# Normalisations laid between the low parts of q and k, row maxima ten steps ahead instead of eight, ten of sixteen moves on GpSimd, and block 6 transposed by VectorE

## The reference

```python
xn = _layernorm(x)
q, k, v = split(xn @ w_qkv);  q, k = spectral_filter(q, mask), spectral_filter(k, mask)
attn = softmax(q @ k.T / 4)                       # 2 batches x 16 heads, 2048 x 2048 each
a = (attn @ v) @ w_out + b_out
y = square(relu(xn @ W_fc.T)) @ W_proj.T          # then 5 steps: mem = 0.9*mem + y - reset
return x + a + mean_of_spikes(y)
```

## Time and profile before

| | |
|---|---|
| median of 3 runs | 1691.74 us (1691.41 to 1691.75) |
| the profiled execution | 1691.07 us, its span 1689.3 us |
| busy in the span | PE 1681.4, PEld 1145.9, DVE 1494.2, ACT 1330.1, POOL 719.7 us |
| granted TensorE clock | 1.00 of full speed |
| first pass, TensorE | 12.09 to 111.37 us |
| score loop | 112.80 to 1658.6 us |
| output projection | 1658.6 us to the end |

### The profile page before, as it was taken

One profiled execution on the slowest core, in us unless ns is written; L12 is line 12 of the kernel. 1 busy time (PEld: TensorE's weight loads), 2 busy tenths in 40 slices (PEclk: granted clock), 3 DMA queues, 4 the chain that ended last, 5 costly groups with the idle time before them and its releaser, 6 DMA issues.

```text
span 1689.3 us, 44435 instructions
## 1 busy us (share of the span) xinstructions
PE 1681.4 (100%) x17842; PEld 1145.9 (68%) x17842; DVE 1494.2 (88%) x2375; ACT 1330.1 (79%) x1718; POOL 719.7 (43%) x979
## 2 busy tenths in 40 slices
PE   9999999999999999999999999999999999999999
PEld 6566666666666666666666666666666666666667
DVE  6889999998999999989998999999989998999884
ACT  5548888888888888888888888888888888888872
POOL 3103334555433345554333455543335554333455
PEclk9999999999999999999999999999999999999999
DMA  6851122112211221122112211221122112211133
GB/s 216 294 161 47 33 54 55 51 33 55 55 50 34 55 55 43 41 55 55 43 41 55 56 37 47 55 55 36 48 55 56 31 53 55 55 30 54 43 105 103
DMA packets 95406, 108.02 MB, mean 64 GB/s; under 512 B 56032, under 2 KB 70240, under 8 KB 95200
## 3 DMA queue, kind: packets, MB, share of 16 engines
q1 hardware_dynamic: 91744, 101.97, 21.2%
q10 hardware_dynamic: 3456, 3.21, 0.6%
HBM read 78.91 MB, written 20.97 MB: 59 GB/s over the span
## 4 chain that ended last, share of the span: by engine, by line
PE 98%; DVE 1%; ACT 0%; issue 0%; ACTq 0%; POOL 0%; POOLq 0%
PE banks L735 31%; PE ring L711 22%; PE ring L718 14%; PE ring L724 14%; PE banks L841 7%; PE banks L846 3%; PE banks L659 2%; PE ring L928 2%; PE ring L672 1%; PE ring L645 1%; PE ring L659 1%; PE ring L686 0%; DVE stats L947 0%; DVE attnT L979 0%; ACT xnT L513 0%
## 5 line engine op out<-in xcount | busy, mean ns | idle before, releaser
L562 ACT ACTIVATE probs<-ring 128x1024 f32<-128x1024 f32 x1024 | 1002.1, 1026 | 6.5 <-PE ring L724 6.2
L711 PE MATMUL ring<-kst,qst 64*128 64x512 f32 x2000 | 674.7, 417 | 0.3 <-ACT probs L562 0.3
L735 PE MATMUL banks<-probs,vst 128*32 128x256 f32 x8192 | 548.2, 385 | 0.1
L1036 DVE TENSOR_REDUCE pmax<-ring 128x2 f32<-128x1024 f32 x407 | 497.7, 1223 | 12.7 <-PE ring L711 0.5
L568 ACT ACTIVATE half_sb<-ring 128x512 f32<-128x512 f32 x500 | 299.2, 598 | 261.4 <-PE ring L711 254.1
L718 PE MATMUL ring<-qst,kst 64*128 64x512 f32 x2048 | 493.0, 425 | 0.1
L711 PEld LDWEIGHTS ring<-kst,qst 64*128 64x128 f32 x2000 | 328.3, 184 | 208.3 <-issue 204.6
L1017 DVE TENSOR_REDUCE pmax<-ring 128x1 f32<-128x512 f32 x500 | 345.4, 691 | 88.7 <-PE ring L711 85.1
L724 PE MATMUL ring<-shift_rows,ones 64*128 64x512 f32 x2048 | 422.9, 390 | 0.0
L1023 DVE TENSOR_REDUCE pmax<-half_sb 128x1 f32<-128x512 f32 x500 | 335.5, 671 | 37.0 <-ACT half_sb L568 33.1
L735 PEld LDWEIGHTS banks<-probs,vst 128*32 128x32 f32 x8192 | 213.7, 109 | 209.7 <-issue 91.0
(11 more groups left out here) (96 smaller groups left out, 1050.9 us busy)
## 6 DMA issues: line engine op xcount, KB each, us to landing
kst<-qk_scratch SPq DMA_DIRECT2D x256, 128.0 KB, 3.0
qst<-qk_scratch SPq DMA_DIRECT2D x256, 128.0 KB, 2.9
qk_scratch<-attnT SPq DMA_DIRECT2D x32, 256.0 KB, 3.0
shift_rows<-shiftT SPq DMA_DIRECT2D x512, 2.0 KB
qk_scratch<-probs SPq DMA_DIRECT2D x16, 256.0 KB, 3.0
attnT<-o_turned SPq DMA_DIRECT2D x256, 16.0 KB, 1.9
xnT<-x SPq DMA_DIRECT2D x8, 512.0 KB, 5.6
out<-xnT SPq DMA_DIRECT2D x7, 512.0 KB, 2.9
```

The source lines that it names most:

```text
L562: act.activation(probs[:, s % PS, :], score_slot(g), ACT.Exp, scale=SCALE).then_inc(exp_done, 1)
L711: return pe.matmul(unit_slot(g)[:, c * BLK:(c + 1) * BLK], qst[b][rows, tile * P:(tile + 1) * P], kst[b][rows, key:key + BLK], start=True, ...
L735: mm = pe.matmul(po[32 * j:32 * (j + 1), half * D:(half + 1) * D], vst[b][:, kt, :], quarters[:, j], start=(kt == 0), stop=(kt == TB - 1))
L1036: dve.tensor_reduce(pmax[:, tile, 2 * part:2 * part + 2], unit_slot(g).rearrange("p (c e) -> p c e", c=2), AX, ALU.max).then_inc(mx_taken, 1)
```

## The change

Five edits in one.

- `LEAD` becomes 10. The first pass takes 44 maxima instead of 48 (`first_max` does nothing from 44 on), and in the last head one more pair, `s` = 8, has maxima. `split_shift` stays at `s` = 10 and 26; `turn_output` goes from 12 and 28 to 14 and 30.
- `TURNED` takes in block 6: VectorE transposes it, and TensorE does so only for blocks 0 and 7.
- `MOVES` becomes (0, 2, 2, 2): ScalarE moves 6 pieces of each such block, GpSimd 10.
- In blocks 1 to 4 the normalisation of block `t + 2` is laid behind the four low parts, the transposition behind the last. Block 0 still normalises block 2 at its end, and block 4 still block 7.
- ScalarE takes the root for block `t + 2` behind high copy 1 in blocks 1 to 4.

```diff
-LEAD = 8
+LEAD = 10
...
-TURNED = range(1, 6)
-MOVES = (0, 2, 3, 3)
+TURNED = range(1, 7)
+MOVES = (0, 2, 2, 2)
...
-                    if t == 4 and w == 1:
-                        deviation(6)
+                    if 1 <= t <= 4 and w == 1:
+                        deviation(t + 2)
                     if t + 1 in TURNED and MOVES[w]:
                         move_turned(t + 1, w)
                 if t < NB - 1 and t + 1 not in TURNED:
                     take_transposed(t + 1)
-                if t < 4:
-                    deviation(t + 2)
+                if t == 0:
+                    deviation(2)
...
             def first_max(n):
+                if n >= FIRST_MAX:
+                    return
...
                     low_part(t, w)
-                    if t == 4 and w < 3:
-                        (block_stats, block_rstd, block_scale)[w](6)
-                if t < 4:
-                    normalise(t + 2)
+                    if 1 <= t <= 4 and (w < 3 or t + 2 in TURNED):
+                        (block_stats, block_rstd, block_scale, turn_block)[w](t + 2)
+                if t == 0:
+                    normalise(2)
...
-            halve(1, pmax[:, TB // 2:TB, 0:2], FIRST_MAX)
+            halve(1, pmax[:, TB // 2:FIRST_MAX // 2 - TB // 2, 0:2], FIRST_MAX)
...
-                if s == LEAD + 2:
+                if s == LEAD:
                     for link in range(4):
-                        split_shift(link, 2 * i + 1, 1, FIRST_MAX + g - 2)
+                        split_shift(link, 2 * i + 1, 1, FIRST_MAX + g)
                 if s == LEAD + 4 and i:
                     turn_output(2 * i - 1)
...
-                if s == LEAD + TB + 2 and not last:
+                if s == LEAD + TB and not last:
                     for link in range(4):
-                        split_shift(link, 2 * i + 2, 0, FIRST_MAX + g - 2)
+                        split_shift(link, 2 * i + 2, 0, FIRST_MAX + g)
                 if s == LEAD + TB + 4:
                     turn_output(2 * i)
```

More of the change, by code:

```diff
@@ L1186, in head @@
                             end_bias_of(t)
-                    if last and s == LEAD + TB:
+                    if last and s == TB + 8:
                         for t in END_LATE:
                             end_bias_of(t)
-                    if last and LEAD + TB < s <= LEAD + TB + 12:
-                        end_base_of((s - LEAD - TB) // 2 - 1)
+                    if last and TB + 8 < s <= TB + 20:
+                        end_base_of((s - TB - 8) // 2 - 1)
             for h in range(H - 1):
```

## The result

The changed kernel takes 1694.45 us in the median of 22 runs (1691.79 to 1695.59), the kernel before 1691.41 in 22 runs on the same chip (1690.69 to 1692.11). The ratio is 1.0016 with a 95% interval of 1.0010 to 1.0022: slower by about 2.7 us, 3.0 by the medians, where I had forecast no change and a range that ended at 1693.6. The profiled execution took 1693.99, its span is 1692.2 against 1689.3.

The account below looks back on a forecast made before the run. TensorE bounds the kernel, 98% of its chain, so only its work and waits count. Reduction +0.92, transposes -0.38, maxima -0.92, last head +0.23 and shift +0.1 sum to -0.05: 1691.7 us, range 1689.7 to 1693.6.

Parts of the forecast that it names:

- Block 2 gets its wait: First pass: block 2 waits for a chain of VectorE and ScalarE work and starts at 34.5 against 33.38, +1.1.
- Eight transposes of block 6: First pass, v of block 5: TensorE drops 0.87 of transposes but 0.49 of cover goes too, -0.38.
- the four maxima: First pass: four maxima less, 0.23 each, -0.92.
- that term: Last head: the shift's transfers land at 1638.5, pair 16 asks at 1638.46, a tie costed at +0.1 (0 to 0.5).
- VectorE reaches the first maxima later: First pass: the first reduction starts at 70.15, `first_max(2)` moves by +0.92, and TensorE's wait grows from 1.44 to about 2.1.
- the third rival: First pass: GpSimd's moves slow down beside VectorE, block 2 starts 2.7 later, reduction +2.6, 1694.3; chance 0.07.
- ends in that wait: First pass: all of the interleaving's gain is lost in TensorE's wait at `first_max(2)`, as block 7's normalisation stays undivided.
- The last head: Last head: pair 8 gets maxima, pairs 8 and 10 take 5.60 instead of 5.37, +0.23 (0 to 0.48).
- The sum: Whole kernel: 0.92 - 0.38 - 0.92 + 0.23 + 0.1 = -0.05, giving 1691.7.
- the forecast's own range: Whole kernel: 1690.1 to 1693.4 for the main forecast, which had chance 0.72.
- The base of the forecast: Whole kernel: the profiled execution's 1691.07, with the median of the runs 0.67 above it.

Follow-up runs that it names:

- the version without them: The changed kernel with block 6 transposed by TensorE again, so no moves lie beside block 7's normalisation: 1691.06 us, ratio 1.0002 to the kernel before.
- the moves held back: The changed kernel with GpSimd's ten moves of block 6 held until block 7 is normalised: 1693.83 us, ratio 1.0008 to the kernel before.
- the wait filled: The changed kernel with six more matmuls, whose output nobody reads, ahead of `first_max(2)`: 1692.43 us, ratio 1.0009 to the kernel before.
- block 6 alone: The kernel before with only block 6's transposition given to VectorE: 1694.30 us, ratio 1.0019.
- the changed kernel with block 1's root last: The changed kernel, but block 1 keeps root, scale and transposition behind low part 3: 1691.79 us, ratio 0.9999 to the kernel before.
- the interleaving alone: The kernel before with only the interleaved normalisations in blocks 1 to 4 and the earlier root: 1693.66 us, ratio 1.0010.
- the moves alone: The kernel before with only `MOVES` = (0, 2, 2, 2), ten moves on GpSimd: 1691.42 us, ratio 1.0002.

## Why the prediction was wrong

**What was right.** Block 2 gets its wait: 34.40 for 34.5, released by ScalarE's move. Blocks 3, 4 and 5 don't wait; block 5 starts at 65.47 for 65.46. Low part 0 of block 4 starts at 57.69, to the hundredth. Eight transposes of block 6 give -0.36 for -0.38, the four maxima -0.91 for -0.92, and v of block 5 is 5.80 long for 5.8. No shift transfer is late at pair 16, so that term is 0 for +0.1, and the loop's pairs with maxima are 3.03 as before.

**Step "VectorE reaches the first maxima later", the size.** I had +0.92 and a wait of about 2.1; it is +1.46 and 2.77. Of the missing 0.54, 0.51 is block 7's normalisation beside GpSimd's ten moves: 5.11 instead of 4.60 in the version without them and 4.56 with the moves held back. I had asked only whether GpSimd slows down beside VectorE, the third rival, and its moves did not (4.58 / 10 = 0.46 each). The contention ran the other way, onto the engine that ends the wait. I had costed block 6's moves by what waits for them, and not by what lies beside them. The trace of before held a small sign of it: with GpSimd's eight moves beside it (58.08 to 61.71), one step of block 6's root chain takes 0.29, and the same step of block 7's, with none beside it, 0.16.

```profile
61.42 0.29 DVE L965 TENSOR_TENSOR rstd<-rstd 128x4 f32<-128x4 f32 x1
...
67.33 0.16 DVE L965 TENSOR_TENSOR rstd<-rstd 128x4 f32<-128x4 f32 x1
```

**The same step, what was left out: the clock.** This is the error that decided. I took a wait of 2.1 as 2.1 us of lost time and nothing more. Behind it the clock falls to 1.2 GHz, and the work that follows pays 1.32 more in the profiled execution, 1.55 and 2.97 in the two others. So the loop's first maximum came at 114.23, where I had 112.4: 0.54 of it is the size above, 1.32 the clock. With the wait filled, the falls are gone. The profile of before shows a clock of 1.00 throughout with a wait of 1.44 in it; I had extended that to a longer wait without a term or a rival for it. The sentence that the interleaving's gain "ends in that wait" should have raised the question.

**The last head.** +0.48 instead of +0.23: pair 8 is 3.03 as said, but pair 10 takes 2.82 and not 2.56. Its scores still wait for an exponential that ScalarE starts at 1632.79, behind a feed-forward copy; the wait that I thought belonged to the missing maxima belongs to that.

**The sum again.** With the measured terms at full clock: +1.46 - 0.36 - 0.08 - 0.91 + 0.48 = +0.6, and the six runs at full clock stand 1692.23 - 1691.41 = +0.8 over before. That lies inside the forecast's own range. The 16 of 22 runs with a fall stand 2.5 higher than those six; in the three profiles the work behind `first_max(2)` takes 1.32, 1.55 and 2.97 more. The base of the forecast, 1691.74 from three runs, lay 0.33 above the 1691.41 beside the changed kernel. I had also taken 3.4 us as the least change that can be told; with 22 runs each, the interval of the ratio is 1 us wide to either side.

**What stays open.** The runs with a fall stand 2.5 over those without in the changed kernel, 2.3 in block 6 alone and 2.2 in the held moves, but 1.1 in the changed kernel with block 1's root last, 1.1 in the interleaving alone and 0.9 in the moves alone. The traces show 1.3 to 1.7 for one short stretch at half clock. No two profiles of one kernel with and without a fall were taken, so where the other part lies isn't shown. It is also open why the filled wait, with no fall, stands 1.5 over before and the changed kernel's six runs at full clock only 0.8. Nor is it shown why one execution falls and the next doesn't; with block 6 alone the same kernel gave both, and its one profile has the wait without the fall.

## What to carry to other kernels

A wait of the engine that sets the end is priced twice: by its length, and by the clock of the work behind it. Ask of every edit that lengthens such a wait by a microsecond whether the profile of before shows a wait as long and what the clock did behind it. Where it shows none, give the loss a chance and a size of its own. And cost work that is moved to an idle engine by what it lies beside as well as by who waits for it: here copies that nobody waited for slowed the engine that did hold up the others.

## What the runs showed of the hardware

- TensorE's granted clock fell from 2.4 to 1.2 GHz behind single waits of 1.87 to 2.88 us in a kernel that is otherwise 99% busy, in roughly half to three quarters of the executions, and in none of the 142 executions of versions whose longest wait was 1.57 or less. Six matmuls in the idle time kept it up. Each short stretch at half clock took 1.3 to 1.7 us from the matmuls; the longer one took 3.0.
- GpSimd copies from SBUF to SBUF slowed some VectorE instructions beside them: a 128x4 `TENSOR_TENSOR` from 0.16 to 0.37, a 128x4 `TENSOR_SCALAR` from 0.17 to 0.26, and four 128x256 `TENSOR_SCALAR` from 1.38 to 1.62, while two other 128x4 `TENSOR_TENSOR` stayed at 0.16. The Trainium skill's GPSIMD Engine Reference, under Key points, has contention for VectorE instructions with two SBUF inputs or in a two-port mode. The rows agree in part: it hit one `TENSOR_TENSOR` and not others, and the slowed `TENSOR_SCALAR` have one tensor input; whether they ran in a two-port mode, no row shows.
